# The state recurrence of a selective-scan layer: one three-operand VectorE instruction per head instead of a product and a sum over four heads

## What is computed

```
S = 1 / (1 + dt*k + dt*dt*A)
z = S * (z - dt*A*s + dt*Bz*u)
s = s + dt*z + dt*Bx*u
y = Cz.z + Cx.s
```

## Time and profile before

| what | us |
|---|---|
| median of 3 runs (1346.82 to 1349.2) | 1347.55 |
| the profiled execution, its own time | 1347.47 |
| its span, first to last instruction | 1345.7 |

### The profile page before, as it was taken

The page is one execution under the profiler, slowest core; times in us unless marked ns, Lnnn a source line. Parts: engine busy times, 40 slices in busy tenths (PEclk is TensorE's granted clock), DMA queues, the critical chain, the costliest instruction groups (busy, mean ns, idle before and its releaser), DMA issues. The chain is left out here.

```text
span 1345.7 us, 22918 instructions
## 1 busy us (share of the span) xinstructions
PE 1274.0 (95%) x7806; PEld 706.0 (52%) x7806; DVE 908.2 (67%) x1771; ACT 635.2 (47%) x1536; POOL 590.2 (44%) x939
## 2 busy tenths in 40 slices
PE   7999668999999999998799998999999999999999
PEld 4443224566566566655445445555555556544545
DVE  6999997888988998989301205888787787630100
ACT  3266214555565565565322314666565666532221
POOL 2633314878878878888300001444344354500000
PEclk7999899999999999999899999999999999999999
DMA  2368896555555555557200002000000000000000
GB/s 82 156 258 334 312 398 235 194 181 184 195 183 184 185 185 192 185 185 234 67 0 0 0 0 89 1 2 1 1 1 1 1 1 1 1 1 0 16 0 16
DMA packets 67746, 143.50 MB, mean 107 GB/s; under 512 B 6833, under 2 KB 22833, under 8 KB 64817
## 3 DMA queue, kind: packets, MB, share of 16 engines
q1 hardware_dynamic: 63024, 129.47, 27.3%
q10 hardware_dynamic: 4608, 12.58, 2.4%
HBM read 94.58 MB, written 47.45 MB: 106 GB/s over the span
## 5 line engine op out<-in xcount | busy, mean ns | idle before, releaser
L1806 POOL TENSOR_SCALAR pr<-pr,rs,sg 128x512 f32<-128x512 f32 (+3 forms) x256 | 152.7, 612 | 204.8 <-DVE rs L1711 185.9
L648 PE MATMUL banks<-w_bc,valueT 128*128 128x512 f32 x448 | 210.7, 594 | 2.1 <-DVE pp L986 2.1
L986 DVE TENSOR_TENSOR pp<-banks,rec 128x1024 f32<-128x1024 f32 x128 | 156.1, 1220 | 6.0 <-POOL bp L1082 0.3
L1612 ACT ACTIVATE pr<-banks,nm 128x512 f32<-128x512 f32 (+3 forms) x256 | 132.8, 524 | 20.5 <-DVE nm L1705 17.7
L1705 DVE TENSOR_REDUCE nm<-banks 128x2 f32<-128x1024 f32 (+3 forms) x128 | 105.5, 824 | 4.4
L648 PEld LDWEIGHTS banks<-w_bc,valueT 128*128 128x128 f32 x448 | 76.7, 190 | 59.7 <-issue 55.5
L1600 ACT COPY prT<-banks 128x512 f32<-128x512 f32 (+3 forms) x128 | 54.3, 424 | 112.5 <-PE banks L1481 112.2
L1067 POOL TENSOR_SCALAR_AFFINE_SELECT bp<-bp 128x1024 f32<-128x1024 f32 x64 | 73.6, 1150 | 75.8 <-ACT bp L880 75.3
L1321 DVE TENSOR_TENSOR x<-x,banks 128x256 f32<-128x256 f32 x16 | 6.7, 421 | 148.3 <-PE banks L1232 148.3
L873 ACT COPY qk<-banks 128x512 f32<-128x512 f32 x128 | 75.0, 586 | 64.0 <-PE banks L773 64.0
L1481 PE MATMUL banks<-ident,pr 128*128 128x128 f32 x640 | 96.9, 281 | 2.1 <-POOL pr L1806 0.7
(11 more groups left out here) (240 smaller groups left out, 2420.5 us busy)
## 6 DMA issues: line engine op xcount, KB each, us to landing
rec<-psi SPq DMA_DIRECT2D x126, 512.0 KB, 4.5
psi<-X SPq DMA_DIRECT2D x15, 2048.0 KB, 7.2
det<-w_bc ACTq DMA_DIRECT2D x16, 512.0 KB, 5.0
dd<-det SPq DMA_DIRECT2D x64, 128.0 KB, 4.7
bcs<-xp ACTq DMA_DIRECT2D x16, 256.0 KB, 6.4
w_bc<-in_w_bc SPq DMA_DIRECT2D x4, 1024.0 KB, 11.1
back<-bcs SPq DMA_DIRECT2D x16, 256.0 KB, 5.0
w_bc<-in_f_h SPq DMA_DIRECT2D x4, 1024.0 KB, 7.8
```

What stands on the lines that cost most here:

```text
L648: mm = pe.matmul(bank, m["valueT"][:, c, t * P:(t + 1) * P], w, start=(c == 0), stop=(c == 1))
L986: dve.tensor_tensor(pp[:, q % 2].rearrange("p (a c) n -> p a c n", c=2), sc.unsqueeze(2).broadcast_to([P, 4, 2, HN]), rec[:, n % RL, q % 2 ...
L1612: act.activation(pr[:, n % RP, h, 0:w], S[n % 2][:, h, 0:w], ACT.Exp, bias=nm[:, n % 4, h:h + 1], accum_out=sm[:, m % 3, n % 2, h:h + 1]). ...
L1806: pool.tensor_scalar(row, row, rs[:, n // 2 % 2, n % 2, h:h + 1], sg[:, TPB * b + it, hd:hd + 1], ALU.mult, ALU.mult).then_inc(s["scaled"], 1)
```

## The change

The product with BETA and its sum become one scalar_tensor_tensor for each of the four heads: out = z(last) * BETA[head, j] + s(last) on 2 x 32 = 64 numbers in a lane, both tensor inputs and the output in `X` (SBUF) and the factor, one number in a lane, in PSUM. A step now has the product with C into `T2`, the four new instructions, and the sum for z. `rec` goes up by 6 in a step, and the waits of VectorE, SyncE and GpSimd count in sixes: the product waits for the four of the step before, the first of the four for the sum of the step before, the sum for its own product, and GpSimd for the third of the four in the step after the one that read its slot (before: for that step's product with C).

```diff
--- before.py
+++ after.py
@@ -161,12 +161,13 @@
         T2 = k.bank[0][:].rearrange("p (r c n) -> p r c n", r=2, c=2)
         BETA = k.bank[1][:].rearrange("p (h t) -> p h t", t=P)
         SLOTS = RINGX * STEPS
+        EACH = 2 + G4
 
         def entry(slot, r):
             return X[:, slot].rearrange("p (r c n) -> p r c n", r=2, c=2)[:, r]
 
         def rec_after(block_no):
-            return 4 * STEPS * (block_no + 1)
+            return EACH * STEPS * (block_no + 1)
 
         @block.sync
         def _(sp):
@@ -210,7 +211,7 @@
                 r = i % RINGX
                 for q in (0, STEPS // 2) if i == NBLK - 1 else (0,):
                     n = STEPS // 2 if i == NBLK - 1 else STEPS
-                    sp.wait_ge(s["rec"], 4 * (STEPS * i + q + n))
+                    sp.wait_ge(s["rec"], EACH * (STEPS * i + q + n))
                     sp.dma_start(scratch["psi"][:, 1 + STEPS * i + q:1 + STEPS * i + q + n, :],
                                  X[:, r * STEPS + q:r * STEPS + q + n, :]).then_inc(stored[r], 16)
             for r in range(RINGX):
@@ -297,22 +298,21 @@
                 for q in range(STEPS):
                     j = STEPS * i + q
                     now, last = r * STEPS + q, (r * STEPS + q - 1) % SLOTS
-                    order = (j % 2, 1 - j % 2)
-                    for n, a in enumerate(order):
-                        if j > 0:
-                            dve.wait_ge(rec, 4 * (j - 1) + 3 + n)
-                        if i == 0 and a == 1:
-                            dve.wait_ge(s["alpha"], q + 1)
-                        if a == 0:
-                            dve.tensor_tensor(T2[:, n].rearrange("p c (h n) -> p c h n", n=N),
-                                              BETA[:, :, j].unsqueeze(1).unsqueeze(3).broadcast_to([P, 2, G4, N]),
-                                              entry(last, 0).rearrange("p c (h n) -> p c h n", n=N), ALU.mult).then_inc(rec, 1)
-                        else:
-                            dve.tensor_tensor(T2[:, n], C[:, i % 2, q].unsqueeze(1).broadcast_to([P, 2, HN]),
-                                              entry(last, 1), ALU.mult).then_inc(rec, 1)
-                    for n, a in enumerate(order):
-                        dve.wait_ge(rec, 4 * j + 1 + n)
-                        dve.tensor_tensor(entry(now, 1 - a), entry(last, 1 - a), T2[:, n], ALU.add).then_inc(rec, 1)
+                    if j > 0:
+                        dve.wait_ge(rec, EACH * j - 1)
+                    if i == 0:
+                        dve.wait_ge(s["alpha"], q + 1)
+                    dve.tensor_tensor(T2[:, j % 2], C[:, i % 2, q].unsqueeze(1).broadcast_to([P, 2, HN]), entry(last, 1),
+                                      ALU.mult).then_inc(rec, 1)
+                    if j > 0:
+                        dve.wait_ge(rec, EACH * j)
+                    for h in range(G4):
+                        own = slice(h * N, (h + 1) * N)
+                        dve.scalar_tensor_tensor(out=entry(now, 1)[:, :, own], in0=entry(last, 0)[:, :, own],
+                                                 scalar=BETA[:, h, j:j + 1], in1=entry(last, 1)[:, :, own], op0=ALU.mult,
+                                                 op1=ALU.add).then_inc(rec, 1)
+                    dve.wait_ge(rec, EACH * j + 1)
+                    dve.tensor_tensor(entry(now, 0), entry(last, 0), T2[:, j % 2], ALU.add).then_inc(rec, 1)
 
             dve.wait_ge(s["de_loaded"], 16 * HG)
             dve.wait_ge(s["abT_taken"], 2)
@@ -595,7 +595,7 @@
                 for q in range(STEPS):
                     if i >= 2:
                         j = STEPS * (i - 2) + q + 1
-                        wait_alone(pool, s["rec"], 4 * j + 2 - j % 2, s["Wset"])
+                        wait_alone(pool, s["rec"], EACH * j + G4, s["Wset"])
                     col = abL[:, :, i * STEPS + q]
                     pool.tensor_tensor(C[:, i % 2, q].rearrange("p (h n) -> p h n", n=N),
                                        col.unsqueeze(2).broadcast_to([P, G4, N]),
```

## The result

The changed kernel takes 1376.84 us (median of 4 runs, 1373.24 to 1378.97) against 1347.77 (1346.82 to 1349.2): a ratio of 1.020, interval 1.018 to 1.023. Slower, as forecast, and inside the range of 1355 to 1382, but by 29 us where 17.5 were forecast, and outside 1359 to 1372, which was the range of the forecast's own case. The profiled execution took 1377.53 us, its span is 1375.6.

What follows compares the result with a forecast made beforehand. The recurrence was taken to run at VectorE's own speed, its end arriving together with TensorE's chain. Terms 15.2 + 1 + 1 = +17.2 us on 1347.47 gave 1364.7, forecast 1365 us, own range 1359 to 1372, 8 in 10: 1355 to 1382.

Steps and rivals of the forecast that it cites:

- the forecast's own case: Whole kernel: the summed terms hold, +17.2 us, giving 1365 us with own range 1359 to 1372; chance 0.71.
- The sign and its reason: Recurrence step on VectorE: slower, four small instructions at 0.784 us for 0.665 removed, +15.2 us over 128 steps.
- The full rate: The four instructions: they run at 1.043 ns an element; the skill's half throughput would add 34 us over all steps.
- The read of the factor: The four instructions: reading a factor for each lane costs 57 ns, not hidden; PSUM priced like SBUF, bounds -29 and +29 us.
- Copies on GpSimd: +1: Recurrence: seven GpSimd one-input operations or memsets hold up VectorE instructions with both inputs in SBUF, 0 to 4.5 us, taken +1.
- Rows 10: Evidence against the port rival: line 963 took 0.18 us while a GpSimd product ran until 0.12 us after its start.
- GpSimd's products hold the port: Rival, recurrence: GpSimd's product holds the product with C, 0.14 to 0.18 us in each of 112 steps: 1383 us; chance 0.08.
- The end: The 192 matmuls after the recurrence: TensorE idles some 15 us before phi, clock may fall; bounds 0 and +5.5, taken +1.
- Everything after moves as a whole: 0: Sections after front: they shift together, unchanged in length, 0 us.
- The lopsidedness: End of the recurrence: later moves the end one for one; earlier brings nothing unless TensorE's own chain comes earlier too.
- The rival that ends faster: Recurrence: factor's read hidden or free from PSUM, spacing 0.139 us, kernel 1343 us; chance 0.08 for over 0.2% faster.
- the dearer factor: Rival, the four instructions: the factor costs up to 57 ns more each from PSUM, up to 1394 us, halfway 1379; chance 0.10.

Runs made afterwards that it cites:

- const_factor: The changed kernel with a constant 0.01 in place of BETA as the factor of the four instructions: 1350.89 us.
- factor_sbuf: The changed kernel with BETA first copied to SBUF by ScalarE, and the four instructions reading their factor there: 1371.53 us.
- one_of_256: The changed kernel with one instruction of 256 elements, using the first head's factor for all, in place of four of 64: 1351.13 us, ratio 1.001.
- two_of_128: The changed kernel with two instructions of 128 elements, each using one head's factor for two, in place of four of 64: 1347.62 us.

## Why the prediction was right, and where it was off

- **The sign and its reason held**: two instructions of 256 elements for four of 64, 0.665 us out and four starts in. The spacing was put at 0.196 us and measured 0.200, the duration at 269 to 283 ns and measured 276, the step at 1.45 and measured 1.467: 17.4 us for a forecast of 15.2, inside the ends. (The group's mean of 289 ns holds the delays.) The full rate held too, at 1.04 ns an element. The read of the factor, worked out as 57 ns and not hidden, is 65 ns (const_factor), and PSUM adds 4 ns of them where I had bounds of -57 and +57.
- **The term that failed is "Copies on GpSimd: +1" (0 to 4.5)**: the delays grew by 7.1 us. Its one-input operations cost 2.7 us, inside the bounds; the 5.2 us beside its products were put at nothing. I had taken that from line 311 alone, which 16 products on GpSimd left at 0.42 us, and read it as "products do not hold VectorE". They do, to their end, where both of VectorE's inputs are in SBUF and GpSimd starts first. In the trace before, line 311 had started first each time and it was GpSimd that gave way: the same products took 0.45 us each there and 0.40 in the changed kernel. I looked at one side of a contest for a port only. Rows 10 fit as well: line 963 ended 0.06 us after GpSimd's product.
- **The rival "GpSimd's products hold the port"** had the mechanism. What it lacked is that the held instruction's start goes on meanwhile: the 0.13 us that the product with C shares with GpSimd's in the steady step, close to the 0.14 of its low bound, fall within its start and cost nothing. That is luck, as nothing in the forecast foresaw it: const_factor, with 0.06 us more, pays. The rule of the Trainium skill (SBUF — State Buffer, "SBUF: two separate sides"), that such a pair locks each other out for a whole instruction, which the prediction held to be refuted for products, is what these runs show for products as for copies: a held scalar_tensor_tensor of 64 elements ended 0.08 us after the end of either.
- **The end**: +1 forecast, 2.2 measured, all of it the clock. That TensorE would idle was right, but it idled 28.0 us and not 15: `phi` was done at 227.05 and not at 220, and TensorE's own chain ended at 199.1, 4.9 us earlier than before. The term was taken near its low end because the clock stayed at a mean of 0.83 with idle times of at most 7.5 us; in this longer one it stayed low.
- **"Everything after moves as a whole: 0"** is right for the work and left out the scatter of the clock: 4.6 us in the profiled execution, 0 in others of nearly the same kernel (the tail from mix on was 1131.3 in factor_sbuf).
- **The lopsidedness**, that a shorter recurrence would bring nothing, was shown by one_of_256 and two_of_128, whose recurrences were 14.8 and 10.3 us shorter. The rival that ends faster was priced at 1343 and needed the spacing of const_factor, 0.135 us; that kernel came to 1350.9 beside 1350.8 for the one before, since collisions ate what the spacing gave.
- **The range** of 8 in 10 held the result because it reached up to take in the port and the dearer factor. The result came there by a sum of small terms, of which the 4.6 us of the tail are chance.

No run was faster than the kernel before beyond its scatter.

## What to carry to other kernels

Count starts before elements: on VectorE here each instruction costs 0.06 to 0.07 us beside its elements, and one that reads a factor for each lane twice that, so a fused operation pays only where it does not have to be cut into pieces. Before speeding up a loop, look at what else arrives at its end: when two chains end within 0.1 us of each other, slower costs everything and faster nothing. And when two engines may share a port, compare the durations on both of them, alone and together, and look at which of the two starts first.

## What the runs showed of the hardware that I had not expected

GpSimd and a VectorE instruction with both inputs in SBUF exclude each other, but only the elements wait. In the narrow windows the first to start keeps its time; a held scalar_tensor_tensor ends 0.08, 0.15 or 0.28 us after GpSimd's instruction (64, 128 or 256 elements), a held product with C 0.29 us, and a held GpSimd product 0.26 us after VectorE's. An overlap of up to 0.13 us with the product with C therefore costs nothing, and neither does any beside a VectorE sum with an input in PSUM. A fall of the granted clock in 28 us of idle TensorE took 2.2 us from 192 small matmuls. The later sections, which the change doesn't touch, took 1131.1 to 1136.3 us from one profiled execution to the next, with the granted clock; what decides when it falls there stays open.
